# 16-wide attentions: contexts divided without being turned, their denominators inverted in a compact layout and repeated over partitions by DMA

## The reference

```
def attention16(x):                       # layers 0, 2, 3; 32 heads of 16
    q, k, v = project(x)                  # layer 0: 8 kv heads, biases, RoPE; 2: 32 kv heads, biases; 3: 8 kv heads
    scores = einsum('bqhd,bkhd->bhqk', q, k) * scale
    scores = where(causal, scores, -big)
    probs = softmax(scores, axis=-1)      # exp(scores - max) / sum
    ctx = einsum('bhqk,bkhd->bqhd', probs, v)
    return ctx @ Wo (+ bo)

x = layernorm(x + attention(x)); x = layernorm(x + ffn(x))   # four times
```

## Time and profile before

| | |
|---|---|
| median of 3 runs | 1924.47 us (1923.56 to 1924.92) |
| profiled execution, its own time | 1924.28 us |
| its span | 1922.6 us |
| busy share PE / DVE / ACT / POOL | 95% / 59% / 45% / 45% |
| mean granted TensorE clock | 0.993 |
| instructions | 29645 |

### The profile page before, as it was taken

How to read it: one execution, slowest core, us unless ns; L and a number is a source line. 1 busy time by engine, 2 the same in 40 slices (tenths; PEclk the granted TensorE clock), 3 DMA queues, 4 the chain that set the end, 5 groups by cost and what they waited for, 6 DMA issues and landing times.

```text
span 1922.6 us, 29645 instructions
## 1 busy us (share of the span) xinstructions
PE 1828.2 (95%) x10760; PEld 1287.9 (67%) x10760; DVE 1130.6 (59%) x2433; ACT 859.2 (45%) x1896; POOL 871.5 (45%) x1383
## 2 busy tenths in 40 slices
PE   7999999999999999999999899999999999999998
PEld 3454447888888888888888687764455454555466
DVE  5677467666666666666666424235556355666465
ACT  1566544444444444444444433314466502565441
POOL 2465426555555555555554444323355312444352
PEclk9899999999999999999999999999999999999999
DMA  7213000101010101010100234205123104211101
GB/s 230 55 46 114 2 18 1 55 1 56 1 55 1 56 1 56 1 56 1 56 1 33 83 115 148 88 1 129 52 69 100 47 1 94 54 36 46 53 10 45
DMA packets 47201, 99.28 MB, mean 52 GB/s; under 512 B 8011, under 2 KB 36043, under 8 KB 43595
## 3 DMA queue, kind: packets, MB, share of 16 engines
q1 hardware_dynamic: 44464, 95.02, 15.6%
q10 hardware_dynamic: 2592, 2.36, 0.5%
HBM read 66.36 MB, written 2.10 MB: 36 GB/s over the span
## 4 chain that ended last, share of the span: by engine, by line
PE 76%; DVE 12%; ACT 4%; issue 3%; DMA 1%; POOL 1%; ACTq 1%; PEld 0%; SPq 0%; PEldq 0%; POOLq 0%; DVEq 0%
PE PS L1483 10%; PE PS L1582 9%; PE PS L485 6%; PE PS L2005 5%; PE PS L595 5%; PE PS L574 4%; PE PS L620 4%; PE PS L1560 4%; PE PS L1544 3%; DVE NM L801 3%; PE PS L2018 3%; PE PS L539 3%; PE PS L1512 3%; PE PS L1976 2%; PE PS L500 2%
## 5 line engine op out<-in xcount | busy, mean ns | idle before, releaser
L1023 ACT ACTIVATE PB<-PS 128x512 f32<-128x512 f32 x480 | 276.4, 600 | 213.1 <-PE PS L574 210.3
L929 POOL TENSOR_SCALAR_AFFINE_SELECT PB<-PB 128x256 f32<-128x256 f32 (+1 forms) x480 | 173.7, 369 | 283.6 <-ACT PB L1023 274.6
L801 DVE TENSOR_REDUCE NM<-PS 128x2 f32<-128x1024 f32 x192 | 206.8, 1090 | 147.3 <-PE PS L541 143.8
L574 PE MATMUL PS<-KQ 99*128 99x512 bf16 (+3 forms) x768 | 179.1, 305 | 9.3 <-ACT PB L1023 4.6
L1774 ACT CAST OTH<-PS 128x512 fp32r<-128x512 f32 x64 | 37.6, 587 | 309.5 <-PE PS L1565 309.5
L1901 POOL TENSOR_SCALAR PR<-PR,RCP 128x512 f32<-128x512 f32 (+3 forms) x256 | 135.5, 540 | 83.3 <-DVE RCP L1704 83.3
L1836 ACT ACTIVATE PR<-PR,NX 128x512 f32<-128x512 f32 (+3 forms) x256 | 145.0, 566 | 32.5 <-DVE NX L1698 29.3
L485 PE MATMUL PS<-XTT,WA 128*128 128x512 f32 x288 | 145.9, 613 | 13.5 <-DVE ident_masks_b L2647 12.0
L1698 DVE CUSTOM_DVE_ANT_0 PR<-PS,CAUSAL 128x512 f32<-128x512 f32 (+3 forms) x256 | 124.3, 486 | 53.3 <-PE PS L1531 52.0
L539 PE MATMUL PS<-KQ 99*128 99x128 bf16 (+2 forms) x576 | 125.2, 278 | 22.6 <-DVE NM L801 20.5
L1662 DVE TENSOR_TENSOR PTL<-PS,PTH 128x384 fp32r<-128x384 f32 (+2 forms) x256 | 115.5, 452 | 28.3 <-ACT PTH L1767 25.9
(11 more groups left out here) (333 smaller groups left out, 4578.4 us busy)
## 6 DMA issues: line engine op xcount, KB each, us to landing
KQ<-HI SPq DMA_DIRECT2D x90, 128.0 KB
KQ<-MID SPq DMA_DIRECT2D x72, 128.0 KB
WB<-f_w SPq DMA_DIRECT2D x12, 768.0 KB, 4.4
WB<-w1o SPq DMA_DIRECT2D x8, 1024.0 KB, 7.9
WC<-f_w SPq DMA_DIRECT2D x10, 768.0 KB, 4.4
WB<-w1a SPq DMA_DIRECT2D x8, 768.0 KB, 4.3
WB<-w1b SPq DMA_DIRECT2D x8, 768.0 KB, 5.8
WA<-w SPq DMA_DIRECT2D x6, 1024.0 KB, 6.4
```

The lines of the kernel that those rows point to most:

```text
L574: x = pe.matmul(ps[:, at:at + T - j * P], KQ[0:PR16, self.key(s, h), j * P:(j + 1) * P], KQ[0:PR16, self.query(s, h), j * P:T], start=True ...
L801: x = dve.tensor_reduce(nm[:, h:h + 2, i], PS[:, b:b + 2, 0:(i + 1) * P], AX.X, ALU.max, negate=True)
L929: pool.affine_select(blocks, blocks, [[0, count], [1, P]], ALU.is_ge, 0.0, base=0, channel_multiplier=-1).then_inc(s16["probs_ready"].sem, 1)
L1023: act.activation(PB[:, n % PBS, :], PS[:, 4 + n % 2, :], ACT.Exp, scale=self.scale)\
```

## The change

For groups 0 to 13 of each attention (`TURNED = 14`) the context is no longer turned to be divided. `back`, `norm` and `ctx_T` stay for groups 14 and 15, the last chunk.

- When `OT` holds the group's contexts and sums, `spread(G)` on SP issues five DMAs: the 4 x 512 sums to `SUMS`, 16 on each of 128 partitions, and the 16 context rows of each of four heads to their place in `XTT`, undivided.
- `invert(C)` on DVE takes one reciprocal of the 128 x 32 sums of a pair of groups, in odd steps after `maxima(s + 2, 1)`.
- `gather_inverse(C)` on SP brings them back to 8 rows of 512 (`INV`) with two DMAs, and `spread_inverse(C)` repeats each row over 16 partitions (`SPREAD`, 128 x 512) with one.
- `scale_ctx(C)` on DVE multiplies the chunk in `XTT` by `SPREAD`, in even steps after `maxima(s + 2, 1)`; the one for `C = 6` comes in step 15.
- `take_out(G)` waits in addition for the DMAs of `spread(G - 1)`, and `pv(G)` waits for `outT_ready` instead of `ctx_ready`; only `pv(15)` still waits for `norm(14)`.

The core of the diff:

```diff
@@ pv
-                    pe.wait_ge(on["ctx_ready"].sem, on["ctx_ready"].at(G))
-                    if G % 2 == 0:
-                        pe.wait_ge(on["ctxT_ready"].sem, on["ctxT_ready"].at(G // 2))
+                    pe.wait_ge(on["outT_ready"].sem, on["outT_ready"].at(G))
+                    if G > TURNED:
+                        pe.wait_ge(on["normed"].sem, on["normed"].at(TURNED // 2 + G - TURNED))
@@ tensor
-                        if k == 1 and s >= 3 and s % 2:
-                            self.ctx_T(pe, (s - 3) // 2, 7)
-                        if k == 8 and s:
+                        if k == 8 and s > TURNED:
                             self.back(pe, s - 1)
@@ vector
+            def invert(self, dve, C):
+                dve.wait_ge(on["out_loaded"].sem, on["out_loaded"].at(160 * (C + 1)))
+                dve.reciprocal(SUMS[:, :, :], SUMS[:, :, :]).then_inc(s16["normed"].sem, 1)
+            def scale_ctx(self, dve, C):
+                dve.wait_ge(on["inv_loaded"].sem, on["inv_loaded"].at(48 * (C + 1)))
+                dve.tensor_tensor(XTT[:, b, c, :], XTT[:, b, c, :], SPREAD[:, :], ALU.mult)\
+                   .then_inc(s16["ctxT_ready"].sem, 1)
-                    if s:
+                    if s > TURNED:
                         self.norm(dve, st, s - 1)
+                if a == 1 and s >= 3 and s % 2:
+                    self.invert(dve, (s - 3) // 2)
+                if a == 1 and s >= 4 and s % 2 == 0:
+                    self.scale_ctx(dve, (s - 4) // 2)
+                if a == 5 and s == NB * GROUPS - 1:
+                    self.scale_ctx(dve, TURNED // 2 - 1)
@@ scalar
+                if 1 <= G <= TURNED:
+                    act.wait_ge(on["out_loaded"].sem, on["out_loaded"].at(80 * G))
                 act.copy(OT[:, :], PS[:, 7, :]).then_inc(s16["outT_ready"].sem, 1)
-                        if k == 1 and s >= 3 and s % 2:
-                            self.take_ctx(act, (s - 3) // 2, 7)
@@ sync
+            def spread(self, sp, G):
+                sp.wait_ge(on["outT_ready"].sem, on["outT_ready"].at(G + 1))
+                sp.dma_start(SUMS[:, e, :], OT[HD:P:32, :]).then_inc(loaded.sem, 16)
+                for h in range(4):
+                    a = 64 * e + HD * h
+                    sp.dma_start(XTT[a:a + HD, b, c, :], OT[32 * h:32 * h + HD, :]).then_inc(loaded.sem, 16)
+            def gather_inverse(self, sp, C):
+                sp.wait_ge(on["normed"].sem, on["normed"].at(C + 1))
+                if C:
+                    sp.wait_ge(on["inv_loaded"].sem, on["inv_loaded"].at(48 * C))
+                for e in range(2):
+                    sp.dma_start(INV[4 * e:4 * e + 4, :], SUMS[:, e, :]).then_inc(s16["inv_loaded"].sem, 16)
+            def spread_inverse(self, sp, C):
+                sp.wait_ge(on["inv_loaded"].sem, on["inv_loaded"].at(48 * C + 32))
+                if C:
+                    sp.wait_ge(on["ctxT_ready"].sem, on["ctxT_ready"].at(C))
+                sp.dma_start(SPREAD[:, :], INV[:, :].unsqueeze(1).to_broadcast([8, HD, T]))\
+                  .then_inc(s16["inv_loaded"].sem, 16)
-                for G in range(1, NB * GROUPS):
-                    self.load_max(sp, G)
+                for G in range(1, NB * GROUPS + 1):
+                    if G >= 4 and G % 2 == 0:
+                        self.gather_inverse(sp, (G - 4) // 2)
+                    if G < NB * GROUPS:
+                        self.load_max(sp, G)
+                    if G >= 4 and G % 2 == 0:
+                        self.spread_inverse(sp, (G - 4) // 2)
+                    if 2 <= G <= TURNED + 1:
+                        self.spread(sp, G - 2)
+                    if G == NB * GROUPS:
+                        break
```

More of the change, by code:

```diff
@@ L371, in build @@
         PB = sb("PB", [P, PBS, T], F32, A16)
-        CTX = sb("CTX", [P, 2, NT, P], F32, A16)
+        CTX = sb("CTX", [P, NT, P], F32, A16)
         OT = sb("OT", [P, T], F32, A16)
@@ L382, in build @@
         RC = sb("RC", [P, NT, 4], F32, A16)
+        SUMS = sb("SUMS", [P, 2, 16], F32, A16)
+        INV = sb("INV", [8, T], F32, A16)
+        SPREAD = sb("SPREAD", [P, T], F32, A16)
         A16.close()
@@ L389, in build @@
         AUX = 6
+        TURNED = NB * GROUPS - 2
         s16 = {k: sig("a16_" + k) for k in (
@@ L812, in norm @@
                 on = self.on
-                dve.wait_ge(on["out_psum"].sem, on["out_psum"].at(G + 1))
+                dve.wait_ge(on["turned_psum"].sem, on["turned_psum"].at(G + 1 - TURNED))
                 o = PS[:, 7, :].rearrange("p (t h e) -> p t h e", t=NT, h=4)
                 st.link(dve.reciprocal(RC[:, :, :], o[:, :, :, HD]))
-                if G >= 4 and G % 2 == 0:
-                    dve.wait_ge(on["ctxT_psum"].sem, on["ctxT_psum"].at(G // 2 - 1))
-                c = CTX[:, G // 2 % 2, :, G % 2 * 64:G % 2 * 64 + 64].rearrange("p t (h e) -> p t h e", e=HD)
+                c = CTX[:, :, G % 2 * 64:G % 2 * 64 + 64].rearrange("p t (h e) -> p t h e", e=HD)
                 dve.tensor_tensor(c, o[:, :, :, 0:HD], RC[:, :, :].unsqueeze(3).to_broadcast([P, NT, 4, HD]),
-                                  ALU.mult).then_inc(s16["ctx_ready"].sem, 1)
+                                  ALU.mult).then_inc(s16["normed"].sem, 1)
+            def invert(self, dve, C):
+                on = self.on
+                dve.wait_ge(on["out_loaded"].sem, on["out_loaded"].at(160 * (C + 1)))
+                dve.reciprocal(SUMS[:, :, :], SUMS[:, :, :]).then_inc(s16["normed"].sem, 1)
+            def scale_ctx(self, dve, C):
+                on = self.on
+                b, c = divmod(C, NC)
+                dve.wait_ge(on["inv_loaded"].sem, on["inv_loaded"].at(48 * (C + 1)))
+                dve.tensor_tensor(XTT[:, b, c, :], XTT[:, b, c, :], SPREAD[:, :], ALU.mult)\
+                   .then_inc(s16["ctxT_ready"].sem, 1)
             def vector(self, dve, st):
@@ L1029, in take_ctx @@
                 b, c = divmod(C, NC)
-                act.wait_ge(on["ctxT_psum"].sem, on["ctxT_psum"].at(C + 1))
-                if c == 0:
-                    act.wait_ge(on["proj_psum"].sem, on["proj_psum"].at(self.each * (b + 1)))
-                    act.wait_ge(on["v_psum"].sem, on["v_psum"].at((b + 1) * (NT if self.wide else 1)))
+                act.wait_ge(on["turned_psum"].sem, on["turned_psum"].at(3))
                 act.copy(XTT[:, b, c, :], PS[:, bank, :]).then_inc(s16["ctxT_ready"].sem, 1)
@@ L1108, in load_max @@
                   .then_inc(s16["max%d_loaded" % (G % 2)].sem, 16)
+            def spread(self, sp, G):
+                on = self.on
+                C, e = divmod(G, 2)
+                b, c = divmod(C, NC)
+                if c == 0 and e == 0:
+                    sp.wait_ge(on["proj_psum"].sem, on["proj_psum"].at(self.each * (b + 1)))
+                    sp.wait_ge(on["v_psum"].sem, on["v_psum"].at((b + 1) * (NT if self.wide else 1)))
+                sp.wait_ge(on["outT_ready"].sem, on["outT_ready"].at(G + 1))
+                loaded = s16["out_loaded"]
+                sp.dma_start(SUMS[:, e, :], OT[HD:P:32, :]).then_inc(loaded.sem, 16)
[3 more added lines that the diff above has]
+            def gather_inverse(self, sp, C):
+                on = self.on
+                sp.wait_ge(on["normed"].sem, on["normed"].at(C + 1))
[4 more added lines that the diff above has]
+            def spread_inverse(self, sp, C):
+                on = self.on
+                sp.wait_ge(on["inv_loaded"].sem, on["inv_loaded"].at(48 * C + 32))
[3 more added lines that the diff above has]
+                  .then_inc(s16["inv_loaded"].sem, 16)
             def load_rows(self, sp, m):
```

17 lines of the change are left out of this document (10 added, 7 removed).

## The result

| | before | changed |
|---|---|---|
| median | 1924.01 us (4 runs) | 1949.89 us (1946.54 to 1952.55, 4 runs) |
| profiled execution | 1924.28 us | 1952.55 us |
| span | 1922.6 us | 1950.8 us |
| mean granted clock | 0.993 | 0.982 |

The ratio is 1.0144, with a 95% interval of 1.0132 to 1.0156. The change makes the kernel 26 us slower. I had forecast 1920.0 us, with a range from 1911 to 1930.

What follows compares the result with a forecast made beforehand. PE, busy 95% of the span, was taken as the bound. From 1924.28 us: -13.8 gain, +6.0 A3's stop, +2.2 its clock, +0.5 A0's end, +0.5 SP gave 1919.7, rounded to 1920.0 us; range 1911 to 1930.

Steps and rivals of the forecast that it cites:

- The gain: Turns of back and ctx_T leaving PE's chain in A0, A2 and A3: 13.8 us, from 7.5 to 14.9.
- the next longest path: A chain that loses a piece may meet another path: 1.1 us taken off the 14.9 us gain.
- The half gain: Rival: ACT or DVE set the pace once PE is relieved, gain half as large, 1926.0 us; chance 0.20.
- The step that failed: The 256 KB SPREAD transfer was priced at 2.6 us from the row of B, sister of f_b.
- the upper bound of 9.5 us: Upper end for SPREAD's landing time, taken from the longest transfer row; the lower end was 1.8 us.
- room: At A2's end the output product lies between, leaving about 2.6 us more before pv(15) waits.
- The rival of slow landings: Each landing takes 4 us instead of 1.8, delaying the attentions' ends: 1932.0 us; chance 0.15.
- The cover of `load_max`: In A0, load_max lands at t + 10.6 and is needed at t + 11.8: 1.2 us to spare.
- The term for SP's queue: Delay of load_max behind SP's new issues in A0 and A3: 0.5 us in all, from 0 to 4.
- The ends: pv(15) waits for norm(14) behind scale_ctx(6): 0.5 us in A0, none in A2, 6.0 in A3.
- The rival in which A3's end does not wait: The 8 KB gather lands early despite f_b; A3 pays 0.5 us and no clock: 1912.0 us; chance 0.20.
- The clock: After A3's stop PE runs at the 1.2 GHz level for a while: 2.2 us, from 0 to 3.4.

Runs made afterwards that it cites:

- inv_apart: The changed kernel with INV's eight rows on partitions 0, 4, ... 28 instead of 0 to 7: 1927.93 us, ratio 1.0045 to the kernel before.
- all_three: The changed kernel with INV's rows apart, A3's last prefetch behind the last SPREAD, and A2's spread(8) behind group 11's maxima: 1919.16 us, ratio 0.9991.
- DRAM: Form of the separate transfer program: 128 rows of 2 KB, 256 KB, read once from device memory: 2.7 us.
- the probe: A separate program that computes nothing: SP issues transfers and waits for each, with different source rows; 256 KB forms took 2.3 to 11.4 us.
- ONE: Form of the separate transfer program: 8 rows moved once, 16 KB: 2.0 us.
- fb_behind: The changed kernel with INV's rows apart and A3's last prefetch, with f_b, issued behind the last SPREAD: 1924.81 us, ratio 1.0018.
- APART: Form of the separate transfer program: 8 rows on partitions 0, 4, ... 28, each read 16 times, 256 KB: 3.7 us.
- ALL: Form of the separate transfer program: 128 rows inside SBUF, each read once, 256 KB: 2.3 us.
- near_three: The changed kernel, INV on partitions 0 to 7, with f_b behind the last SPREAD and A2's spread(8) behind group 11's maxima: 1941.74 us, ratio 1.0104.
- two_copies: The all_three kernel with OT in two buffers in turn, so a group's copy waits for the rows of the group before the last: 1911.36 us, ratio 0.9956.

## Why the prediction was wrong

**The gain was near.** I took 13.8 us. In `inv_apart`, where the slow transfer doesn't blur them, the falls from group to group sum to 4.1 us in A0 (groups 0 to 14), 4.8 in A2 (0 to 8, and 10 to 14) and 4.3 in A3, 13.2. But A3 gives 3.5 us back at its groups 5, 7 and 9 (1.6 in `all_three`), so that 9.7 are left (11.2 in `all_three`). In `all_three` the chain runs there over POOL, which splits the maxima that `max_T` (L556) turns:

```profile
1714.93 0.76 POOL NM L940
...
1715.73 0.23 PE PS L556
```

At this place of the kernel before it went from DVE's maximum to PE:

```profile
1720.61 1.24 DVE NM L801
...
1722.73 0.14 PE PS L551
```
 I had taken 1.1 us off for the next longest path, and had named ACT and DVE for it, not POOL. Why POOL is late there was not tried. The half gain, 7.5 us, is refuted.

**The step that failed** is "The trace shows no SBUF transfer of 256 KB; `f_b`'s sister `B` with 256 KB took 2.6, which I take for `SPREAD`". It took 7.0. The row was a load from device memory, like DRAM in the probe (2.7), and I carried its time over to a transfer whose 128 rows come from eight. I gave the upper bound of 9.5 us and then let no rival use it. Put into my own working it is 4.4 us more at A0's end, 1.8 at A2's, whose room is 2.6, and 4.4 at A3's, 10.6 together; the runs show 10.4. The rival of slow landings had this sign and the late landing at the ends; but it made all three landings slower, while the gathers took about the 1.8 us that I had (ONE in the probe: 2.0), and its price was 12 us, where the place of the rows cost 22.

**What the prediction did not have** is the hold. I costed each issue at 0.63 to 0.73 us, and the one behind a SPREAD takes 4.2 us at its longest. The cover of `load_max` that I put at 1.2 us in A0 is gone by that alone. The term for SP's queue was 0.5 us, with 4 as its upper end; A0's group 12 alone cost 4.6. I did name `load_max` as what is queued behind SP's new waits, but then looked only for the longest row of issues, in A0, and left out the wait that the diff adds for the reuse of XTT. In A2 it stands ahead of `load_max(11)` for 9.4 us, and cost 7.9 us with SPREAD fast. That is about as much as the 7.3 us by which the kernel with the rows apart is still slower than the one before.

**The ends.** A0's: 0.5 us forecast, 6.5 measured, 1.6 with the rows apart. A2's: 0, 2.3, 0.0. A3's: 6.0 and 2.2 for the clock forecast, 12.1 measured, 8.9 with the rows apart, so this term was right in mechanism and near in size: `inv_apart` shows 6.65 us of stop and 2.2 of slow `pv`. `fb_behind` shows the queueing. The rival in which A3's end does not wait is refuted.

**The clock.** I charged it at one place. The changed kernel pays it behind two stops: 1.9 us at A3's end and 1.5 at A0's (`pv` of 4.22 and 3.83 us instead of 2.29). How much of PE's further busy time comes from the stops, and how much from chance, was not tried.

**What stays open**: the 1.4 us between APART and ALL; why the place of the rows costs 5.0 us at A2's group 8 in `near_three` and 2.6 in the changed kernel; and how much of the 22 us is clock and how much is wait, since the two come together.

## What to carry to other kernels

Before you let a DMA repeat a few rows over all partitions, ask on which partitions these rows lie: eight neighbours took 7.1 us for 256 KB, eight rows four partitions apart 3.7. Give a transfer a price from a row with the same kind of source, and where there is none, let the upper bound be a rival with its own chance. A queue that issues for several consumers should have nothing in front of the most urgent one that waits for something far off: neither a large load (8 KB waited 5 us behind 1152 KB) nor a reused buffer (9.4 us in A2).

## What the runs showed of the hardware that I had not expected

- A slow transfer holds its issuer: behind one of 256 KB from 8 neighbouring partitions four issues took 6.11 us instead of some 2.4, and in the kernel a single one up to 4.2 us.
- The same transfer in two halves is slower, not faster: 11.4 us against 7.1.
- Rows 16 partitions apart (WIDE, 4.3 us) are worse than rows 4 apart (3.7).
- Where nothing was changed, the time still moves with PE's clock: ahead of A0's first copy the executions differ by up to 4.8 us (`fb_behind` and `two_copies`, whose granted clocks over the first 60 us are 0.96 and 1.00).
